# The order of three pieces of TensorE work in a cross-attention slot

## The reference, cut to what matters

```
q = layernorm(x) @ Wq.T + bq            # 256 x 512
k = ctx @ Wk.T + bk ;  v = ctx @ Wv.T + bv   # 4096 x 512
scores = clip(q @ k.T / sqrt(32), -50, 50), masked
p = softmax(scores);  out = (p @ v) @ Wo.T + bo ...
```

## Time and profile before

| | |
|---|---|
| median of 3 runs | 716.76 us (716.7 to 716.88) |
| the profiled execution | 716.85 us, its span 714.7 us |
| busy share of the span | PE 98%, PE weight loads 64%, DVE 85%, ACT 61%, POOL 2% |
| chain that ended last | PE 62%, DVE 29%, ACT 4%, issue 4%, DMA 1% |
| granted TensorE clock | 1.0 |
| slots 0 to 55 of the cross-attention | 34.14 to 277.39 us |

### The profile page before, as it was taken

The page is one execution under the profiler, slowest core; times in us unless marked ns, Lnnn a source line. Parts: engine busy times, 40 slices in busy tenths (PEclk is TensorE's granted clock), DMA queues, the critical chain, the costliest instruction groups (busy, mean ns, idle before and its releaser), DMA issues.

```text
span 714.7 us, 20508 instructions
## 1 busy us (share of the span) xinstructions
PE 699.3 (98%) x8722; PEld 455.1 (64%) x8722; DVE 610.2 (85%) x946; ACT 435.5 (61%) x598; POOL 11.6 (2%) x36
## 2 busy tenths in 40 slices
PE   8999999999999998998999999999999999999998
PEld 3555555555555554546777767777777777777775
DVE  5689999999999999787889977888888888888885
ACT  4778888787878886735677753444444344444442
POOL 3000000000000000010000000000000000000000
PEclk9999999999999999999999999999999999999999
DMA  8560101010110000032334403667677776767770
GB/s 322 174 276 3 62 3 62 6 58 14 50 30 36 2 3 3 2 138 87 112 122 155 161 1 103 226 216 249 221 245 227 238 235 231 244 223 244 223 244 32
DMA packets 29880, 94.44 MB, mean 132 GB/s; under 512 B 5824, under 2 KB 15088, under 8 KB 28400
## 3 DMA queue, kind: packets, MB, share of 16 engines
q1 hardware_dynamic: 28944, 92.31, 38.7%
q10 hardware_dynamic: 864, 1.07, 0.5%
HBM read 92.76 MB, written 0.57 MB: 131 GB/s over the span
## 4 chain that ended last, share of the span: by engine, by line
PE 62%; DVE 29%; ACT 4%; issue 4%; DMA 1%; POOL 0%; DVEq 0%; ACTq 0%
PE pS L1227 35%; PE pP L1227 12%; PE pD L1227 8%; DVE arena L898 7%; PE pO L1227 5%; DVE x_sb L907 4%; DVE arena L907 4%; DVE xT L907 4%; DVE xn L907 3%; DVE arena L758 2%; DVE arena L764 2%; ACT arena L566 2%; DMA arena<-in_ctxT 1%; ACT arena L527 1%; PE pO L1622 1%
## 5 line engine op out<-in xcount | busy, mean ns | idle before, releaser
L1227 PE MATMUL pS<-arena 128*128 128x256 f16 (+3 forms) x2185 | 253.5, 272 | 1.9 <-ACT arena L591 0.8
L1227 PEld LDWEIGHTS pS<-arena 128*128 128x128 f16 (+1 forms) x2185 | 213.1, 101 | 46.0 <-ACT arena L623 1.9
L1227 PE MATMUL pP<-arena 128*32 128x512 f16 (+1 forms) x2996 | 239.8, 380 | 0.7 <-ACT arena L467 0.7
L1227 PEld LDWEIGHTS pP<-arena 128*32 128x32 f16 (+1 forms) x2996 | 109.1, 97 | 102.0 <-issue 2.2
L527 ACT ACTIVATE arena<-pS,mblk 128x1024 f32<-128x1024 f32 x112 | 128.9, 1206 | 4.9 <-PE pS L1227 4.7
L1053 DVE SCALAR_TENSOR_TENSOR arena<-arena 128x1536 f16<-128x1536 f32 x72 | 126.1, 1752 | 0.8 <-ACT arena L667 0.8
L707 ACT ACTIVATE arena<-pS 128x256 f32<-128x256 f32 x72 | 27.7, 384 | 154.1 <-PE pS L1227 154.1
L1227 PE MATMUL pO<-arena 128*32 128x256 f32 (+6 forms) x1370 | 106.8, 357 | 2.6 <-DVE arena L1048 2.0
L667 ACT ACTIVATE arena<-arena 128x1536 f16<-128x1536 f32 x72 | 106.4, 1477 | 1.0 <-PE pP L1227 1.0
L898 DVE TENSOR_SCALAR arena<-arena 128x1024 f32<-128x1024 f32 x112 | 73.3, 689 | 7.4 <-ACT arena L527 7.4
L1227 PE MATMUL pD<-arena 128*128 128x512 f16 x288 | 77.8, 379 | 0.0
(11 more groups left out here) (252 smaller groups left out, 520.0 us busy)
## 6 DMA issues: line engine op xcount, KB each, us to landing
arena<-in_units SPq DMA_DIRECT2D x72, 768.0 KB, 4.7
arena<-w_scratch SPq DMA_DIRECT2D x136, 64.0 KB, 2.7
arena<-in_ctxT SPq DMA_DIRECT2D x7, 1024.0 KB, 5.2
mw_in<-in_mla_in SPq DMA_DIRECT2D x8, 832.0 KB, 7.0
mw_out<-in_mla_out SPq DMA_DIRECT2D x8, 512.0 KB, 3.6
wlatT<-in_wlatT SPq DMA_DIRECT2D x1, 1280.0 KB, 10.7
arena<-in_ctxT ACTq DMA_DIRECT2D x4, 256.0 KB, 6.1
arena<-in_wkT SPq DMA_DIRECT2D x4, 256.0 KB, 5.7
```

Source lines behind the costliest of these rows:

```text
L1227: return pe.matmul(o, lhsT, rhs, start=start, stop=stop, **kw)
```

## The change

In x_block of TensorE's program, project is put ahead of weigh. The order of a slot becomes scores, project, weigh, in all slots of blocks 0 to 6 that have both. The clearing in slot 0 of block 0 stays ahead of project, add_sums in slot 3 of block 6 follows weigh and so comes behind project, and last_block, ACT, DVE, POOL and the DMA queues are untouched.

```
                 for i in range(PAIRS_X):
                     scores(b, p, i)
+                    if first and i == 0:
+                        pe.wait_ge(s["proj_evac"], 8)
+                        add_zero((pO[:, 0, :], pO[:, 1, :], pD[:, :]), True, False)
+                    if not (b == NBLK - 2 and i == PAIRS_X - 1):
+                        project(b + 1, 1 - p, i)
                     if i:
                         weigh(b, p, i - 1)
-                    elif first:
-                        pe.wait_ge(s["proj_evac"], 8)
-                        add_zero((pO[:, 0, :], pO[:, 1, :], pD[:, :]), True, False)
-                    else:
+                    elif not first:
                         weigh(b - 1, 1 - p, PAIRS_X - 1)
                     if b == NBLK - 2 and i == 3:
                         add_sums(b, 0)
-                    if not (b == NBLK - 2 and i == PAIRS_X - 1):
-                        project(b + 1, 1 - p, i)
```

## The result

The changed kernel takes 717.75 us in the median of 20 runs, the kernel before 716.70 in 20 runs beside it: ratio 1.0018, 95% interval 1.0012 to 1.0025. That is about a microsecond slower, as forecast (717.7): the interval leaves out 1, and 1.0018 is just inside the 0.2% that was taken as no change.

A forecast was written before the change was run, and what follows sets the result against it. TensorE, never idle in slots 0 to 54, sets the pace. Slot 1's 0.66 stall less slot gains makes DVE 0.60 late, slot 48 makes TensorE 1.28 late, the end +0.98: median 717.7 us, 8-in-10 range 716.5 to 718.9.

The forecast's parts named there:

- No wait of TensorE to remove: Slots 0 to 54: TensorE is busy 239.92 of 239.92 us, so more room for DVE's clips is worth 0.
- The order inside a slot: Every slot's shape changes: two either way, so a slot gains 0 to 0.02 us, taken as 0.01, 0.54 over 54.
- The rival of a drain from f16 to f32: Project ahead of weigh: array drains, 54 x 0.12 = 6.5 us, total about 723.7; chance 0.06.
- The copy out of pP: Slot 1: only scores lies between the first two projects, so project waits for the copy, a new 0.66 us stall.
- The clock of DVE: From slot 7's exponential, where DVE's free run starts, DVE is 0.60 us late throughout.
- The context quarter: First slots of blocks: project waits for the last L758; the largest, in slot 48, decides, leaving TensorE 1.28 us late.
- What the end gives back: Slots 52 and 53: earlier copies start exponentials 0.89 behind scores, so slot 53's, DVE and last_block move +0.98 us.
- Rival 1: Context waits of successive blocks add up because TensorE's waits push DVE on: +2.6 us, 719.4; chance 0.12.
- The total: Whole kernel: last_block and all behind it move +0.98 us, 716.85 to 717.83 profiled, forecast median 717.7.

The follow-up runs named there:

- e4_all: Changed kernel with slots 1 to 4 in the old order, the last context quarter split before the additions, and ACT's two moves: 715.51 us against 716.78, ratio 0.9986.
- e1: Changed kernel with the old order kept in slots 1 to 4 of block 0: ratio 1.0011 to the kernel before.
- e6: Changed kernel with the old order in slot 0 of blocks 1 to 6: ratio 1.0049 to the kernel before.
- e2: Changed kernel with DVE's split of a block's last context quarter put ahead of the additions in slot 7: ratio 1.0002 to the kernel before.
- e3: Changed kernel with ACT's bias copies moved from slot 48 to 54 and one weight split from slot 52 to 53: ratio 1.0013 to the kernel before.
- e5: Kernel before, in its old order, with only the DVE context-split edit and ACT's two moves: 716.40 us against 716.78, ratio 0.9994.
- e0_after: The changed kernel as it is, run again beside the first experiments: ratio 1.0019 to the kernel before.

## Why the prediction was right, point by point

- *No wait of TensorE to remove.* Right. A wait for DVE's clips would differ from slot to slot, as DVE's distance does; in e4_all every slot is shorter by the same 0.02.
- *The order inside a slot.* The sign was right, the size was not: 0.0235 us per slot where 0.01 was taken, just above the upper bound of 0.02, 1.27 us over 54 slots instead of 0.54. Both parts of the sum were a little off. Averaged over the slots without a wait, project behind scores takes 2.600, only 0.008 above its 12 x 0.216 = 2.592, where weigh took 0.888, 0.024 above its 4 x 0.216 = 0.864. And weigh ahead of scores takes 0.970, 0.106 on top and not the 0.12 that the sum gave it; project had paid 0.114 there (2.706). The rival of a drain from f16 to f32 is dead: its slots of 4.47 are not there.
- *The copy out of pP.* 0.66 forecast, 0.67 measured, and confirmed from both sides: taken away (e1) and made seven times (e6).
- *The clock of DVE.* +0.60 forecast, +0.51 to +0.52 measured from slot 12 to slot 48. The 0.08 is the mis-sized slot gain over the slots before DVE's free run.
- *The context quarter.* The lateness of TensorE when it enters slot 49 was forecast as 1.28 and is 1.18; waits stand in slots 16 to 48, and they did not add up, as was said: e1 moved both engines together. They sum to 1.6 us, but most of that only takes back what the slots gain. The one claim on them that was wrong is which would be the longest, at about a microsecond: it is slot 40 (0.60) and not slot 48 (0.23). The trace of before shows why. L758 of the last quarter ends 2.77 us after the start of slot 16, then 2.82, 2.88, 3.29 and 3.33 after slots 24, 32, 40 and 48. The step of 0.41 ahead of slot 40 is the 0.46 us that DVE waits for itself, in its work of slot 38, and this wait is there in every kernel:

```profile
205.47 1.22 DVE L907 TENSOR_TENSOR x_sb<-x_sb,arena 128x1024 f32<-128x1024 f32 x1 [0.46 <-DVE x_sb L907]
```

  The prediction knew of this wait and placed it only ahead of slot 48. Slot 40 takes it up, and slot 48 is left with the gain of 8 slots, 0.19, and 0.04.
- *What the end gives back.* This is the step that failed in part. It let TensorE run from slot 49 to 53 without a stall. ACT's queue was checked only where it holds the exponentials, not where it holds the copy of pP: the bias copies in slot 48 and the weight splits in slot 52 now stand between exponentials and a copy that project reaches sooner. That added stalls of 0.35 in slot 49 and 0.20 in slot 53. Only the first moves the end: it brought the exponentials of slot 53 to 268.04 - 0.37 = 267.67 instead of 267.46, and the end to +1.17 instead of +0.98. The stall in slot 53 stands behind that slot's scores, and so behind the exponentials that set the end. The runs bear this out: in every kernel but e4_all the end is TensorE's lateness at the scores of slot 53 less 0.25, to 0.04 us, since the exponentials start 0.89 behind these scores and not 1.14 (1.44 in the changed kernel, 0.82 in e1, 0.05 in e2, 1.05 in e3, 0 in e5, 3.60 in e6). e3 showed that ACT's queue was the cause.
- *Rival 1, that context waits add up through DVE*: in the changed kernel DVE's lateness is constant to 0.01 from slot 12 to 48, so it did not occur. What it describes does exist: in e6 DVE follows TensorE. Only in slots 50 and 51 of the changed kernel is DVE pushed on, from +0.52 to +1.1.
- *The total* was nearly right, and partly by luck. By the profile it is +1.17 (+1.12 in e0_after) against +0.98. TensorE enters slot 49 0.10 less late than forecast, its four slots from there gain 0.05 more, and the missing stall of 0.35 adds to that: 0.98 - 0.10 - 0.05 + 0.35 = 1.18. The slot gains were too small by 0.7 us, but the waits for DVE take most of that back, so it hardly shows. The medians agree to 0.05 (717.75 against 717.7), closer than the profiles do, because the kernel before came out at 716.70 this time and not at 716.76.

## What to carry to other kernels

When a piece of work moves to the other side of another, look at the first and last repetition: the steady state can keep every distance, and the first pair not, and a single stall there can shift an engine that runs freely for the next forty repetitions. For each signal that the moved piece waits for, compare the new time of need with the end of the producer in every repetition, not in a typical one, and list what stands ahead of the producer in its own queue. An order that is better by 0.5% of a slot paid here only when the places where it comes too early were mended as well. The waits that it meets on the way are not its price one by one: each only brings the fast engine back to the slower one that it depends on.

## What the runs showed that was not expected

A change of the array's shape costs something on both of its sides, and by kind of piece. Behind scores the f32 weigh takes 0.024 us more than its four groups of 0.216, project 0.008 more than its twelve; ahead of scores project takes 0.114 more and weigh 0.106. The two differences, 0.016 and 0.008, are the gain of 0.0235 us per slot.

Two DVE instructions of 0.69 us take 1.29 together when neither waits, so that a wait of 0.40 between them costs 0.49.

A pause of TensorE of 1.9 to 2.0 us far behind the changed code is in all nine profiles; the granted clock falls within 1 us behind it in three of them (after, e3_act_moves, e5_control) and not in the other six.
